# A fused decoder layer on one core: one pattern of step kinds for every job, due times for every engine, two output areas

## What is computed

```python
x = layernorm(x + mamba(mamba(x)))        # two layers, 512 inner channels, 64 states
x = layernorm(x + cross_attention(x, context))
x = layernorm(x + mixture(x))             # 8 experts, hidden 1024, the best 2 per position

# the inner scan of a mamba layer, for each state s and channel d:
h[t] = exp(dt[t] * A[d, s]) * h[t - 1] + dt[t] * u[t] * B[t, s]
y[t] = sum over s of h[t] * C[t, s];  then y = (y + u * D) * silu(z)
```

## Time and profile before

| | |
|---|---|
| Median of 3 executions | 3313.5 us (3312.0 to 3314.0) |
| The profiled execution, its own time | 3315.7 us |
| Its span, first to last instruction | 3313.7 us |
| Head, before the first step's multiplication by C | 40.3 us |
| Sixteen jobs | 3068.9 us |
| Tail, after the last step's multiplication | 204.5 us |
| Mean granted TensorE clock | 0.95 of 2.4 GHz |
| HBM traffic | 313 MB read, 31 MB written |

### The profile page before, as it was taken

How to read it: one execution, slowest core, us unless ns; L and a number is a source line. 1 busy time by engine, 2 the same in 40 slices (tenths; PEclk the granted TensorE clock), 3 DMA queues, 4 the chain that set the end, 5 groups by cost and what they waited for, 6 DMA issues and landing times.

```text
span 3313.7 us, 59014 instructions
## 1 busy us (share of the span) xinstructions
PE 2872.3 (87%) x21490; PEld 2612.5 (79%) x21490; DVE 2977.4 (90%) x2141; ACT 2645.0 (80%) x6150; POOL 2659.4 (80%) x1289
## 2 busy tenths in 40 slices
PE   6999999998898889999868799989777888999776
PEld 4888888887788779888867688878666778888666
DVE  6999999999999989999999999999999999999610
ACT  6879888887888689888978789898887879988422
POOL 4989999898989788887888879887988888877501
PEclk8999999999999899999989899999999989999788
DMA  3342222222222135335211244424211133444276
GB/s 102 102 163 85 69 60 78 64 64 63 71 71 61 55 122 177 111 107 157 93 56 57 74 140 147 159 90 145 69 62 56 48 122 118 136 153 139 85 250 215
DMA packets 264660, 347.51 MB, mean 105 GB/s; under 512 B 88218, under 2 KB 157603, under 8 KB 263988
## 3 DMA queue, kind: packets, MB, share of 16 engines
q1 hardware_dynamic: 260418, 332.98, 31.8%
q0 software_dynamic: 3072, 8.39, 0.7%
q10 hardware_dynamic: 882, 2.38, 0.2%
HBM read 313.03 MB, written 30.62 MB: 104 GB/s over the span
## 4 chain that ended last, share of the span: by engine, by line
PE 31%; POOL 21%; issue 17%; ACT 14%; DVE 14%; DMA 2%; SPq 1%; POOLq 0%; DVEq 0%; ACTq 0%
POOL hC L1012 18%; DVE h L1239 8%; PE psY L1553 8%; PE psG L1492 8%; ACT dA L1207 7%; DVE psX L1229 4%; PE psX L1524 3%; PE psG L1579 3%; PE psX L1534 3%; ACT xs L1178 3%; PE psX L1492 2%; POOL scratch L938 1%; PE psX L1516 1%; ACT hid L1162 1%; POOL dt L949 1%
## 5 line engine op out<-in xcount | busy, mean ns | idle before, releaser
L1012 POOL TENSOR_TENSOR hC<-h,cb 128x1024 f32<-128x1024 f32 x1024 | 2403.4, 2370 | 463.6 <-DVE h L1239 443.2
L1239 DVE TENSOR_TENSOR_SCAN h<-dA,psX 128x1024 f32<-128x1024 f32 (+1 forms) x1115 | 2302.9, 2101 | 77.8 <-PE psX L1524 37.0
L1207 ACT ACTIVATE dA<-dt,negA 128x255 f32<-128x255 f32 x4096 | 1715.9, 502 | 147.8 <-DVE h L1239 143.9
L1553 PE MATMUL psY<-ident,hC 128*128 128x128 f32 x8192 | 1099.1, 279 | 43.0 <-DVE gT L1254 37.2
L1553 PEld LDWEIGHTS psY<-ident,hC 128*128 128x128 f32 x8192 | 958.2, 144 | 51.5 <-DVE gT L1254 40.3
L1229 DVE TENSOR_TENSOR psX<-dtu,psX 128x1024 f32<-128x1024 f32 x443 | 535.6, 1209 | 43.8 <-PE psX L1516 43.2
L1524 PE MATMUL psX<-ident,xs 128*128 128x128 f32 x2992 | 412.6, 283 | 119.3 <-ACT xs L1178 74.8
L1178 ACT ACTIVATE xs<-dtuT,bT 128x512 f32<-128x512 f32 x748 | 497.3, 717 | 2.9 <-PE psX L1524 2.9
L1524 PEld LDWEIGHTS psX<-ident,xs 128*128 128x128 f32 x2992 | 348.5, 145 | 170.2 <-ACT xs L1178 97.7
L1534 PE MATMUL psX<-diag_b,dtuT 128*128 128x128 f32 x3312 | 421.1, 282 | 45.5 <-DVE h L1239 45.0
L1534 PEld LDWEIGHTS psX<-diag_b,dtuT 128*128 128x128 f32 x3312 | 399.3, 196 | 72.9 <-issue 70.3
(11 more groups left out here) (213 smaller groups left out, 2051.8 us busy)
## 6 DMA issues: line engine op xcount, KB each, us to landing
cb<-c_dram SPq DMA_DIRECT2D x256, 512.0 KB
w_up<-in_w_exp SPq DMA_DIRECT2D x201, 256.0 KB
w_down<-in_w_exp SPq DMA_DIRECT2D x201, 256.0 KB, 2.8
diag_b<-b_dram SPq DMA_DIRECT2D x207, 128.0 KB
dA<-in_w_exp SPq DMA_DIRECT2D x39, 256.0 KB, 5.0
h<-in_w_exp SPq DMA_DIRECT2D x39, 256.0 KB, 4.9
x_slots<-got SPq DMA_DIRECT2D x16, 512.0 KB, 4.9
xg<-x_slots SPq DMA_DIRECT2D x60, 128.0 KB, 2.8
```

What stands on the lines that cost most here:

```text
L1012: eng.tensor_tensor(hC[i % NHC][:, :, :], h[i % NH][:, :, :], cw.to_broadcast([P, KI, L]), ALU.mult).then_inc(times_c, 1)
L1207: made = eng.activation(dA[j % NA][:, c, 1:L], dt[n % 2][:, c, 1:L], ACT.Exp, scale=negA[:, JOBS[n][0], c, s:s + 1])
L1239: made = eng.tensor_tensor_scan(h[i % NH][:, part, :].rearrange("p c t -> p (c t)"), dA[i % NA][:, part, :].rearrange("p c t -> p (c t)"), ...
L1553: made = eng.matmul(psY[:, tc, c * P:(c + 1) * P], hC[i % NHC][:, c, tc * P:(tc + 1) * P], ident[:, :], start=s == 0 and c == 0, stop=s == ...
```

## The change

All late jobs take the early pattern. The planner gets other costs, ends that lie behind an instruction's issue time (`END`, `FILL_END`), and `latest`, which goes back over the next five or so steps and gives for TensorE, ScalarE and GpSimd the latest time at which they may still be at other work, with a margin. The next job's transposed dt*u is forced into the lists four steps ahead of the job (`force`). y_slots becomes two areas used in turn, so that clearing takes 32 transfers of 512 KB for 24, and the first tile of a pair is stored after the fetches of the pair before the last. In the tail SP's stores and loads of rows 4 and 5 are moved behind the sixth tile of the last pair.

The diff without small edits: the loop's model takes the new ends and hops for the old costs throughout, `kind_of` gives a step's kind (plain outside the loop), and these costs change, in ns: resid1 and resid2 2000 to 2350, prob 1300 to 650, top 1100 and 900 to 1200 and 1000, weights 1100 to 1000, logit_exp 220 to 150, xg_copy 440 to 290, relu 4 x 260 to 4 x 250, blend 900 to 970, bn3 1400 to 1720.

```diff
@@ -50,9 +50,8 @@
 PLAIN, ROWS_SCALED, BY_MATRIX = "PTM"
 MATRIX_FROM = 24
 EARLY = "PMT" * 21 + "P"
-LATE = "PTPMPTPTPMTPTPT" * 4 + "PTPM"
 FIRST_JOB = "P" * 13 + "TP" * 5 + "T" + EARLY[MATRIX_FROM:]
-KINDS = FIRST_JOB + EARLY * 5 + LATE * (NJ - 6)
+KINDS = FIRST_JOB + EARLY * (NJ - 1)
 KINDS = KINDS[:-1] + PLAIN
 assert len(KINDS) == STEPS
 NDIAG = 4
...
 Task = namedtuple("Task", "piece eng ns needs opens frees")
-MM, TURN, EVICT, HALF_EVICT = 450, 112, 500, 360
-WINDOW, PE_OVER, FIRST, LONG, HOP, NEAR = 24, 0, 1500, 3300, 100, 60
+MM, HID_MM, TURN, EVICT, HALF_EVICT = 432, 448, 109, 490, 360
+WINDOW, FIRST, LONG, HOP = 24, 1500, 3300, 60
 SKIP_FROM = S // 2
-PRESS_FROM, PRESS = 44, 300
+PRESS_FROM, PRESS = 36, 60
 KEEP = 4
-SUM, SPREAD, OUTER, MULTIPLY, SCALE, DECAY, TIMES_C, PRODUCT, SCAN, SPLIT = 900, 250, 920, 1830, 1230, 1600, 2330, 1240, 2200, 190
+
+FILL = {PLAIN: 270, ROWS_SCALED: 870, BY_MATRIX: 1790}
+FILL_END = {PLAIN: 410, ROWS_SCALED: 980, BY_MATRIX: 1930}
+SUM, SCALE, DECAY, TIMES_C, PRODUCT, SCAN, SPLIT, GATE = 870, 1230, 1600, 2320, 1240, 2200, 120, 1300
+END = {"PE": 120, "ACT": 100, "DVE": 50, "POOL": 50, "DMA": 0}
+MARGIN = {"PE": 300, "ACT": 300, "POOL": -600}
+FORESIGHT = 5
+DUE = 4
 VECTOR_WORK = {"resid1", "norm1", "max", "prob_norm", "resid2", "norm2", "logit_max", "logit_sum", "top", "weights", "place", "list",
...
-        out += [task("y_copy", t, 0, "ACT", 420, ("out", t, (1, 3)), *((("tile_out", t - 1, 0),) if t else ()), frees=("out", t, (0, 0))),
+        out += [task("y_copy", t, 0, "ACT", 290, ("out", t, (1, 3)), *((("tile_out", t - 1, 0),) if t else ()), frees=("out", t, (0, 0))),
                 task("tile_out", t, 0, "DMA", 2500, ("y_copy", t, 0),
-                     *((("fetched", GROUPS[g - 1][-1], 0),) if g and t == TILE0[g] else ()))]
+                     *((("fetched", GROUPS[g - 2][-1], 0),) if g > 1 and t == TILE0[g] else ()))]
     for b in GROUPS[g]:
...
-        at = max([self.at[t.eng]] + [self.done[x] + (self.hop if self.made_by.get(x) != t.eng else 0) for x in t.needs])
+        at = max([self.at[t.eng]] + [self.done[x] + (END[self.made_by[x]] + HOP if self.made_by[x] != t.eng else 0) for x in t.needs])
...
-                    over = (LONG if t.ns > 4000 else FIRST) + self.press if rank == 0 and t.eng == "ACT" else 0
+                    over = 0
+                    if rank == 0:
+                        over = self.press + ((LONG if t.ns > 4000 else FIRST) if t.eng == "ACT" else 0)
                     if at + t.ns <= limit[t.eng] + over:
...
+    def force(self, where, piece):
+        while piece not in self.done:
+            for chain in self.chains:
+                ready = [(*self.start(t, {"G": "G", "M": "GM"}), t) for t in chain]
+                at, k, t = min((r for r in ready if r[0] is not None), key=lambda r: r[0], default=(None, None, None))
+                if t:
+                    self.place(chain, t, at, k, where)
+                    break
+
...
+    def latest(self, i, then):
+
+        scan_by = {i + 1: then}
+        for j in range(i + 2, i + 4 + FORESIGHT):
+            scan_by[j] = scan_by[j - 1] + SCAN + (0 if is_turned(j) else PRODUCT)
+        pe = act = pool = 1e12
+        for j in reversed(range(i + 2, i + 2 + FORESIGHT)):
+            kind = kind_of(j)
+            pe = min(scan_by[j - 1] - HOP - FILL_END[kind], max(pe, scan_by[j - 1] + HOP) - SUM - FILL[kind])
+        for j in reversed(range(i + 3, i + 3 + FORESIGHT)):
+            kind = kind_of(j)
+            decay_by = scan_by[j - 1] + (PRODUCT if kind == PLAIN else 0) - HOP - DECAY - END["ACT"]
+            if kind == ROWS_SCALED:
+                x_by = scan_by[j - 1] - 2 * HOP - FILL_END[kind] - SCALE - END["ACT"]
+                act = min(x_by, decay_by - SCALE, act - DECAY - SCALE)
+            else:
+                act = min(decay_by, act - DECAY)
+        for j in reversed(range(i + 1, i + 1 + FORESIGHT)):
+            pool = min(scan_by[j + 1] + FILL[kind_of(j + 3)] - TIMES_C - END["POOL"] - HOP, max(pool, scan_by[j + 1] + HOP) - TIMES_C)
+        return {"PE": pe - MARGIN["PE"], "ACT": act - MARGIN["ACT"], "POOL": pool - MARGIN["POOL"]}
...
-                room = then - ((MULTIPLY if is_by_matrix(i + 2) else OUTER) if is_turned(i + 2) else SPREAD) + PE_OVER
-                limit = {"PE": room if i + 1 < STEPS else 1e12, "ACT": then + 500, "POOL": then + 600, "DMA": then + 10000,
-                         "DVE": at["DVE"] + 2100 if i + 1 < STEPS and not is_turned(i + 1) else 0}
+                limit = self.latest(i, then)
+                room = limit["PE"]
+                if i + 1 >= STEPS:
+                    limit = dict.fromkeys(limit, 1e12)
+                limit["DMA"] = then + 10000
+                limit["DVE"] = at["DVE"] + 2500 if i + 1 < STEPS and not is_turned(i + 1) else 0
 
                 self.press = max(0, s - PRESS_FROM) * PRESS
                 self.fill(self.beside[i], limit, at["DVE"])
                 self.keep_busy(i, room)
+                if (i + DUE) % S == 0 and i + DUE < STEPS:
+                    self.force(self.beside[i], ("dtu_copy", n + 1, KL - 1))
...
-        y_slots = nc.dram_tensor("y_slots", [SLOTS, D], F32, kind="Internal").ap()
+        y_slots = [nc.dram_tensor(f"y_slots{i}", [SLOTS, D], F32, kind="Internal").ap() for i in range(2)]
...
-        CLEARS = 3 * SLOTS * D // (P * KL * 2 * D)
+        CLEARS = 4 * SLOTS * D // (P * KL * 2 * D)
...
-                for b in GROUPS[g - 1] if g else ():
+                for b in GROUPS[g - 2] if g > 1 else ():
                     on.wait_ge(fetched[b], 16 * 4)
                 on.wait_ge(cleared, 16 * CLEARS)
-                eng.dma_start(y_slots[bass.DynSlice(tile_combo(t) * P, P), :], yg[:, :]).then_inc(y_tile_out, 16)
+                eng.dma_start(y_slots[g % 2][bass.DynSlice(tile_combo(t) * P, P), :], yg[:, :]).then_inc(y_tile_out, 16)
...
+            def stores_later(pieces):
+                at = pieces.index(("list", ROWS - 1, 0))
+                late = [x for x in pieces[at:] if x[0] in ("norm3", "acc_load") and x[1] in GROUPS[-2]]
+                rest = [x for x in pieces if x not in late]
+                at = rest.index(("out", TILE0[-2] + 5, (1, 3))) + 1
+                return rest[:at] + late + rest[at:]
...
-            small_work(plan.tail)
+            small_work(stores_later(plan.tail))
```

More of the change, by code:

```diff
@@ L70, in is_by_matrix, with kind_of @@
     return 0 <= i < STEPS and KINDS[i] == BY_MATRIX
+def kind_of(i):
+    return KINDS[i] if 0 <= i < STEPS else PLAIN
 MATRIX = [i for i in range(STEPS) if KINDS[i] == BY_MATRIX]
@@ L234, in tasks_row @@
     then("max", 0, "DVE", 900)
-    then("prob", 0, "ACT", 1300, frees=("score", b, 0))
+    then("prob", 0, "ACT", 650, frees=("score", b, 0))
     then("prob_norm", 0, "DVE", 1000)
@@ L243, in tasks_row @@
     then("o", 1, "PE", 3 * MM)
-    then("resid2", 0, "DVE", 2000, frees=("o", b, 0))
+    then("resid2", 0, "DVE", 2350, frees=("o", b, 0))
     then("rstd", 1, "POOL", 700)
@@ L250, in tasks_row @@
     then("logit_max", 0, "DVE", 350, frees=("logit", b, 0))
-    then("logit_exp", 0, "ACT", 220)
+    then("logit_exp", 0, "ACT", 150)
     then("logit_sum", 0, "DVE", 600)
-    then("top", 0, "DVE", 1100)
-    then("top", 1, "DVE", 900)
-    then("weights", 0, "DVE", 1100)
+    then("top", 0, "DVE", 1200)
+    then("top", 1, "DVE", 1000)
+    then("weights", 0, "DVE", 1000)
     then("count", 0, "PE", 1300, opens="G")
@@ L290, in tasks_experts @@
                 before = (("hid", t, (half, i - 1)),) if i else (("hid", t, (0, 3)),) if half else ()
-                out.append(task("hid", t, (half, i), "PE", MM, ("xg_copy", t, 0), *before, opens=None if i else "M"))
+                out.append(task("hid", t, (half, i), "PE", HID_MM, ("xg_copy", t, 0), *before, opens=None if i else "M"))
             used = (("out", t - 1, (half, 3)),) if t else ()
-            out.append(task("relu", t, half, "ACT", 4 * 260, ("hid", t, (half, 3)), *used, frees=("hid", t, (half, 0))))
+            out.append(task("relu", t, half, "ACT", 4 * 250, ("hid", t, (half, 3)), *used, frees=("hid", t, (half, 0))))
         for half in range(2):
@@ L315, in tasks_experts @@
         out.append(task("fetched", b, 0, "DMA", 3500, ("fetch", b, (KL - 1, 1))))
-        out += [task("blend", b, tc, "DVE", 900, ("fetched", b, 0), ("acc_load", b, 0)) for tc in range(KL)]
-        out += [task("bn3", b, 0, "DVE", 1400, ("blend", b, KL - 1), *((("norm3", b - 1, 0),) if b else ())),
+        out += [task("blend", b, tc, "DVE", 970, ("fetched", b, 0), ("acc_load", b, 0)) for tc in range(KL)]
+        out += [task("bn3", b, 0, "DVE", 1720, ("blend", b, KL - 1), *((("norm3", b - 1, 0),) if b else ())),
                 task("rstd", b, 2, "POOL", 700, ("bn3", b, 0)),
@@ L419, in keep_busy @@
                 self.at["PE"] += many * TURN
+    def latest(self, i, then):
[17 more added lines that the diff above has]
```

(13 more changed lines are left out.)

32 lines of the change are left out of this document (17 added, 15 removed).

## The result

The changed kernel takes 3354.4 us (median of 4, 3352.4 to 3356.9) against 3313.1 for the kernel before; the ratio is 1.0123, interval 1.0108 to 1.0138. It is slower by 41 us, where 57 us less was forecast, and lies 9 us above the range. The span of the profiled execution is 3352.1 us, 38.4 more than before.

A forecast was written before the change was run, and what follows sets the result against it. VectorE was taken to bound the loop of scans, with TensorE nearly full; -96.6 (products) - 20 (VectorE waits) - 8 (blending) + 69 (longer tail) - 2 (jobs 3 to 5) = -58 us, forecast 3256, range 3185 to 3345.

The forecast's parts named there:

- The bound and the trade: Late loop runs at VectorE's pace: 96.6 us of products saved, TensorE pays 166, and 114 of expert tiles go to the tail.
- 166 - 35 - 14 = 117: TensorE's work: 166 us more for matrix steps, less 35 from higher clock in late jobs and 14 in the tail.
- the idle time: TensorE idle in jobs 6 to 15: 11 us per job, 110 for ten.
- the 28 us left in the tail: Tail: idle of 27.0 us in its first 61 and 4.4 in the next 20 filled; 24.7 at the end stay.
- The amount of work left over: Nearly all expert tiles of rows 4 and 5, 114 us of TensorE work, left for the tail; 14 or 15 tiles.
- Rival C: Attention starved of plain steps (22 for 30), lists late, jobs 8, 9, 12, 13 stay idle: 3410, half 3333; chance 0.18.
- where 17 was the turning point: Late jobs: a mean TensorE idle of 17 us per job was to decide for lists coming late, which makes it slower.
- Part (2): Twelve more matrices per job stored and loaded through DRAM on SP's queue: costed at nothing, covered by a five-step lead.
- Both signs that I had set against it: VectorE waiting above 10 us for matrix fills, or TensorE waiting for matrix loads, would mean the extra matrices were not free.
- Part (3): Planner's due times, 300 ns margin: VectorE idle 7.6 us per late job, 20 less over ten; forced inputs at no cost.
- Part (4): Two output areas, later stores, a third more clearing: off the path in the loop; clearing nothing, at most a few us.
- rival A: Whole loop: VectorE stays the only bound, TensorE absorbs 17 us per job, tail keeps 204.5: 3195 or 3187; chance 0.15.

The follow-up runs named there:

- experiments 4 and 8: Changed kernel: 4 admits no expert piece on TensorE while an attention piece does not fit, 3287.7 us; 8 instead lets attention's large pieces exceed TensorE's limit, 3290.1 us.
- experiment 2: Changed kernel with the old pattern of step kinds in jobs 6 to 15, all else as changed: 3296.3 us, ratio 0.9955 to the kernel before.
- experiment 7: Changed kernel with expert pieces held back on TensorE while an attention piece does not fit, and the old late pattern in jobs 14 and 15: 3255.5 us.
- experiment 10: experiment 7 with one area for tile outputs, as in the kernel before: 3318.9 us, ratio 1.0029 to the kernel before.

## Why the prediction was wrong

**The bound and the trade were right.** VectorE's products went (362, forecast 363), the late loop follows VectorE, and what TensorE had no time for went into the tail. TensorE's work over jobs 6 to 15 and the tail rose from 1871.4 to 1980.6 us, 109; the forecast was 166 - 35 - 14 = 117. The clock gave back what was counted on where tiles were there: the low clock of job 9 is gone, 1.00 for 0.91, and job 13 has 0.99 for 0.91. So the sign set for being wrong altogether, a late loop not shorter by 90 us, did not come up (91), and yet the kernel is slower.

**The step that failed is the idle time**, "With later due times but a margin I take 11, so 110 for ten jobs", and the 28 us left in the tail. Against the forecast of the span, 96 us are missing: 52 of TensorE's idle time in the late jobs (162 for 110), 47 in the tail (75 for 28), 8 in jobs 0 to 5, less 8 of work and 3 of the head. Of the 52, 43 are jobs 10 and 11. I had taken idle time from jobs where tiles were there, and assumed that they always would be. Of the tail's 47, 26 are the two stops, and 17 the first 81 us with row 7's chain in them, which I had counted as filled.

The amount of work left over was not the error: 13 tiles of the third pair came into the tail (forecast 14 or 15), and the products of the expert tiles there are busy 113 us longer (forecast 114). That it came out is in part luck: the late loop was 33 us longer than forecast, with TensorE 52 us idler in it. (The rest of the 96 by length: 58 in the tail, 5 before job 6.)

**Rival C came nearest, and for the wrong reason.** It had a chance of 0.18 and gave 3333 to 3410 by late lists. Its own sign, 30 us and more of idle in jobs 8, 9, 12 or 13, did not come up (17.7 at most), because the starved jobs were 10 and 11. The mean idle was 16 us per late job, where 17 was the turning point, and the tail's stops did the rest. "Against it: after job 6 there would be a backlog" held for four jobs: the products with expert weights took 29 to 35 us in each of jobs 6 to 9 and used up the first pair's tiles by job 10, with no list behind them. Attention did not lack VectorE's plain steps (experiments 4 and 8); it lacked a hole on TensorE as long as its largest pieces. The forecast did not ask what a tighter limit does to pieces of different length.

**Part (2), matrices at no cost,** held nearly. Both signs that I had set against it came up: VectorE waited 19.7 us for matrix fills, over 10, and TensorE waited for the loads, 9.8 us in three places, all in late jobs.

```profile
PE psX L1593 <- DMA diag_b<-b_dram: 9.8, 3, 3.3
```

So it is some 10 us of the 96 at most; how much of VectorE's waiting is the loads' and how much a late TensorE was not tested. **Part (3)** was half right. What experiment 2 keeps of the change gains 15 us under the old pattern, but under the new one VectorE was idle 112 us in jobs 6 to 15, not 76. And the forced inputs were not free: of those 36 us, 16 are the two waits of 8.1 in jobs 11 and 13. **Part (4)** was wrong twice. stores_later, at nothing in my sum, cost 13 us, since four transfers that wait stood ahead of a tile's output store in one queue. And two areas are not "off the path in the loop" once there is a backlog: taking one away from experiment 7 costs 63 us, 18 of them in the loop (experiment 10). What it would cost in the changed kernel itself no run shows.

**Matmul or weight-load row.** The weight-load rule of the Trainium skill (Trainium Kernel Development and Optimization, Performance Expectations) led to rival A, nothing deferred. In job 8, always supplied, the matmul row leaves 6.9 us of 177.0 and the weight-load row 16.5, and tiles were deferred all the same. Deferral alone does not test the rule, since the planner decides it from its own costs. The full windows in the tail do: from 3235 to 3245 us the matmul row is busy 10.00 of 10 and the weight-load row 9.41. In this kernel, whose TensorE work is mostly float32 products of 128 columns, the matmul row is the one that closes.

## What to carry to other kernels

Where a greedy planner fills one engine from several chains, the urgent chain's largest piece needs a hole; once an engine is nearly full, hold back small pieces of lesser chains while it does not fit. Before trading one engine's time for another's, ask not only whether the sum fits but whether the work that is to fill it will be there in each stretch. And in a queue that issues in order, a store that waits for compute must not stand ahead of transfers on which the engine one is short of depends: here the store whose landing gave an output buffer back.

## What the runs showed of the hardware that was not expected

The order of SP's queue, and not bandwidth, behind the tail's second stop: from 3255 to 3265 us the DMA engines are busy for 0.30 while TensorE stands still. And the clock: the granted clock is 0.62 in that window and 0.53 in the next, and 1.00 from 3280 to 3300. In windows of 2 us it is 0.50 until 3274, 0.90 to 3276 and 1.00 from there, while the matmuls begin again at 3270.3. So a stop of 16 us costs an estimated 2 more in half-speed matmuls behind it, half of 3.7 us and a tenth of 2.
